# Moving a ring's rows and indices: from copies on GpSimd to DMAs issued by SyncE, in a graph network with residual norms

## The reference

```python
x = _layernorm(x + _L0_gnn_ref(x, src, dst))                 # 10 steps of propagation, alpha = 0.1
x = _layernorm(x + _L1_gnn_ref(x, edge_index, w, fc_w, fc_b, bias))   # attention, 4 heads
x = _layernorm(x + _L2_gnn_ref(x, ..., src, dst, edge_type_86))       # 16 basis matrices by type
x = _layernorm(x + _L3_gnn_ref(x, edge_weight, edge_index, 100000))   # weighted sum over edges
```

## Time and profile before

| | |
|---|---|
| median of three runs | 2988.89 us |
| the profiled execution's own time | 2987.88 us |
| its span, first to last instruction | 2986.1 us |
| DVE busy | 2053.3 us, 69% |
| POOL busy | 1783.6 us, 60% |
| ACT busy | 574.2 us, 19% |
| PE busy | 536.1 us, 18% |
| chain that ended last | DVE 39%, issue 22%, POOL 13%, DMA 6%, PE 5%, ACT 3% |
| POOL's copies out of the ring (L716) | 40 into YW, 14.6 us; 12 into RB, 9.3 us |
| DMA queues | POOL's 7.0%, SP's 6.7% of 16 engines' span |

### The profile page before, as it was taken

One profiled execution on the slowest core, in us unless ns is written; L12 is line 12 of the kernel. 1 busy time (PEld: TensorE's weight loads), 2 busy tenths in 40 slices (PEclk: granted clock), 3 DMA queues, 4 the chain that ended last, 5 costly groups with the idle time before them and its releaser, 6 DMA issues.

```text
span 2986.1 us, 24643 instructions
## 1 busy us (share of the span) xinstructions
PE 536.1 (18%) x3578; PEld 339.1 (11%) x3578; DVE 2053.3 (69%) x3755; ACT 574.2 (19%) x1342; POOL 1783.6 (60%) x1893
## 2 busy tenths in 40 slices
PE   4760000047100000000003022320245450000000
PEld 2330000036100000000002011220122220000000
DVE  6777878878863555555899377069778788676662
ACT  6970111113000000000012002431233330101000
POOL 5777777777735265556557777670346460715776
PEclk9995555569555555555556555555555555555555
DMA  6002222200011022222120101011000001000000
GB/s 210 13 12 86 76 72 76 66 22 13 12 55 11 20 21 23 26 20 53 55 52 10 52 11 8 1 52 44 4 6 7 6 8 44 10 2 7 10 9 9
DMA packets 78886, 96.54 MB, mean 32 GB/s; under 512 B 45888, under 2 KB 70640, under 8 KB 76920
## 3 DMA queue, kind: packets, MB, share of 16 engines
q0 software_dynamic: 53664, 20.91, 7.0%
q1 hardware_dynamic: 25176, 75.21, 6.7%
HBM read 38.06 MB, written 60.81 MB: 33 GB/s over the span
## 4 chain that ended last, share of the span: by engine, by line
DVE 39%; issue 22%; POOL 13%; DMA 6%; PE 5%; ACT 3%; DVEq 2%; POOLq 1%; ACTq 1%; SPq 0%
POOL ring L724 4%; POOL cring L465 3%; DMA cring<-sums_by_list,cidx 2%; DVE YW L1180 2%; DVE RB L1180 1%; POOL attention_by_edge L820 1%; PE banks L2580 1%; POOL out_dram L481 1%; POOL ring L813 1%; DVE YW L1017 1%; DVE YW L1011 1%; DVE roots L1008 1%; DVE roots L1018 1%; DVE roots L1012 1%; DVE SW L1300 1%
## 5 line engine op out<-in xcount | busy, mean ns | idle before, releaser
L481 POOL DMA_INDIRECT out_dram<-ring,ridx x196 | 206.1, 1051 | 141.5 <-DVE ridx L2074 82.6
L490 POOL DMA_INDIRECT SW<-node_table,srci x196 | 220.8, 1126 | 64.5 <-issue 64.5
L490 POOL DMA_INDIRECT XS<-in_x_dram,xsi x196 | 202.1, 1031 | 81.6 <-issue 62.3
L490 POOL DMA_INDIRECT XD<-in_x_dram,xdi x196 | 202.7, 1034 | 62.6 <-issue 62.6
L839 POOL DMA_INDIRECT out_dram<-z4w,oidx x98 | 96.2, 982 | 225.2 <-ACT oidx L2334 195.6
L465 POOL DMA_INDIRECT cring<-sums_by_list,cidx x128 | 123.6, 966 | 120.4 <-issue 78.8
L2132 ACT ACT_TABLE_LOAD x42 | 53.9, 1283 | 641.6 <-DVEq L997 641.6
L2367 PE MATMUL banks<-YW 128*128 128x392 f16 x784 | 140.2, 333 | 47.5 <-ACT YW L2154 37.6
L2449 PE MATMUL banks<-tl,dcar 128*128 128x32 f32 (+1 forms) x14 | 4.4, 404 | 799.4 <-DVEq L1290 618.3
L724 POOL DMA_INDIRECT ring<-x_by_edge,aidx x96 | 95.1, 990 | 41.9 <-issue 22.5
L942 DVE TENSOR_SCALAR YW<-YW,b_d 128x784 f16<-128x784 f16 x196 | 83.0, 424 | 49.0 <-PE banks L2367 47.1
(11 more groups left out here) (614 smaller groups left out, 3420.8 us busy)
## 6 DMA issues: line engine op xcount, KB each, us to landing
nx<-in_x_dram SPq DMA_DIRECT2D x10, 625.0 KB
YW<-in_x_dram SPq DMA_DIRECT2D x10, 625.0 KB
out_dram<-nx SPq DMA_DIRECT2D x10, 625.0 KB
out_dram<-YW SPq DMA_DIRECT2D x10, 625.0 KB
sums_by_list<-RB SPq DMA_DIRECT2D x2, 1800.0 KB
sums_by_edge<-RB SPq DMA_DIRECT2D x1, 3528.0 KB, 9.8
sums_by_list<-RB SPq DMA_DIRECT2D x2, 1600.0 KB
XS<-in_x_dram,xsi POOLq DMA_INDIRECT x196
```

The source lines that it names most:

```text
L481: pool.indirect_dma_start(out=table, out_offset=off, in_=ring_row(h, j, w), in_offset=None, bounds_check=limit, oob_is_err=False).then_inc ...
L490: pool.indirect_dma_start(out=dest[:, t * w:(t + 1) * w], out_offset=None, in_=table, in_offset=bass.IndirectOffsetOnAxis(ap=idx[:, t:t + ...
```

## The change

POOL's `fetch_rows` and `put_rows` lose their copies: POOL waits for `moved_s` (or `staged_s`) and issues the indirect DMAs, nothing else. The copies become plain DMAs that SP issues from two new functions: `fetch_moves` writes the landed rows from the ring to the target tile and the next indices into aidx, `put_moves` writes indices and rows into aidx and the ring. A semaphore per half counts 16 for each of these DMAs. SP waits for each half's landing itself.

```diff
+            def fetch_moves(n, idx, dest, moved_s, landed_s, k=0):
+                width = 2 * CU * D
+                def index(h, i):
+                    sp.dma_start(aidx[:, h, 0:CU], idx[:, bass.ds(i * (2 * CU) + h * CU, CU)]).then_inc(moved_s[h], 16)
+                def rows(h, at_, landed):
+                    sp.wait_ge(landed_s[h], landed)
+                    sp.sem_inc(s_tick[4], 1)
+                    sp.dma_start(dest[:, bass.ds(at_, CU * D)], ring[:, h, 0:CU * D]).then_inc(moved_s[h], 16)
+                for h in range(2):
+                    index(h, 0)
+                with sp.Fori(1, n) as i:
+                    for h in range(2):
+                        rows(h, i * width + (h * CU * D - width), (n * (16 * CU) + i * (16 * CU)) if k else i * (16 * CU))
+                        index(h, i)
+                for h in range(2):
+                    rows(h, n * width + (h * CU * D - width), n * (16 * CU * (k + 1)))
+            def put_moves(n, idx, rows, w, staged_s, put_s):
+                def stage(h, i):
+                    sp.dma_start(aidx[:, h, 0:CU], idx[:, bass.ds(i * (2 * CU) + h * CU, CU)]).then_inc(staged_s[h], 16)
+                    sp.dma_start(ring[:, h, 0:CU * w], rows[:, bass.ds(i * (2 * CU * w) + h * (CU * w), CU * w)]
+                                 ).then_inc(staged_s[h], 16)
+                for h in range(2):
+                    stage(h, 0)
+                with sp.Fori(1, n) as i:
+                    for h in range(2):
+                        sp.wait_ge(put_s[h], i * (16 * CU))
+                        sp.sem_inc(s_tick[4], 1)
+                        stage(h, i)
+                for h in range(2):
+                    sp.wait_ge(put_s[h], n * (16 * CU))
+                    sp.sem_inc(s_tick[4], 1)
...
@@ SP's program behind the ten steps
-            write_table(agg_d, 1)
...
             sp.dma_start(e4w[:, :], inv_d.rearrange("(p j) w -> p (j w)", p=P)).then_inc(s_invl, 16)
+            write_table(agg_d, 1)
+            sp.wait_ge(s_tabw, 16)
+            fetch_moves(n0, rows0, YW, s_fst, s_fget)
             sp.wait_ge(s_x1, 1)
             sp.dma_start(dense(x1_d, D), XD[:, :]).then_inc(s_x1w, 16)
+            sp.wait_ge(s_trips[3], 1)
+            ns = sp.value_load(trips_i[3][0:1, 0:1], min_val=1, max_val=CW // (2 * CU))
+            sp.wait_ge(s_qi, 1)
+            fetch_moves(ns, qi, SRD, s_srt[0], s_sget[0])
+            sp.wait_ge(s_agu, 1)
+            fetch_moves(ns, si, SRS, s_srt[1], s_sget[1])
             sp.wait_ge(s_sgo, SINGLES)
             sp.dma_start(dense(att_d, D), S[:, :]).then_inc(s_gw, 16)
...
+            sp.wait_ge(s_dup, 1)
+            put_moves(ns, ti, SA, D, s_tset, s_tput)
             sp.dma_start(S[:, :], dense(attd_d, D)).then_inc(s_attl, 16)
-            for h in range(2):
-                sp.wait_ge(s_dput[h], ns * (16 * CU))
-                sp.sem_inc(s_tick[4], 1)
+            put_moves(ns, qi, SA, D, s_dset, s_dput)
             sp.dma_start(Y, dense(att_d, D)).then_inc(s_al, 16)
             write_table(rgcn_d, 2)
+            sp.wait_ge(s_tabw, 32)
+            fetch_moves(n0, rows0, YW, s_fst, s_fget, 1)
@@ POOL
+            def fetch_rows(n, table, moved_s, landed_s, k=0):
+                with pool.Fori(0, n) as i:
+                    for h in range(2):
+                        pool.wait_ge(moved_s[h], (n * 32 + (i * 32 + 16)) if k else (i * 32 + 16))
+                        pool.sem_inc(s_tick[0], 1)
+                        for j in range(CU):
+                            pool.indirect_dma_start(out=ring_row(h, j, D), out_offset=None, in_=table, ...
+            def rows_moved(moved_s, count): ...   # waits for both halves' moves
+            def put_rows(n, w, table, staged_s, put_s, last): ...   # likewise, waits for i * 32 + 32
```

More of the change, by code:

```diff
@@ L371, in gnn_resnorm @@
         s_x1, s_x1w = sem("x1_dst_ready"), sem("x1_dst_written")
-        s_srt = [sem(f"sorted_{side}_staged") for side in ("dst", "src")]
+        s_srt = [[sem(f"sorted_{side}_moved{h}") for h in range(2)] for side in ("dst", "src")]
         s_sget = [[sem(f"sorted_{side}_landed{h}") for h in range(2)] for side in ("dst", "src")]
@@ L409, in gnn_resnorm @@
         s_expl = sem("list_values_loaded")
-        s_stg = [sem(f"group_staged{k}") for k in range(2)]
-        s_xtp = [sem(f"group_transposed{k}") for k in range(2)]
-        s_xtc = [sem(f"transposed_group_copied{k}") for k in range(2)]
+        s_stg = [None, sem("group_staged")]
+        s_xtp = [None, sem("group_transposed")]
+        s_xtc = [None, sem("transposed_group_copied")]
         s_xy, s_xyu = sem("relation_terms_ready"), sem("relation_terms_used")
@@ L707, in _ @@
             pool.sem_inc(s_tick[0], 1)
[L708 to L714, removed]
-                    pool.sem_inc(s_tick[0], 1)
[L716 to L726, removed]
-                plus = lambda a, b: a + b if k else b
-                for h in range(2):
-                    issue(h, 0, plus(step0, h + 1))
-                with pool.Fori(1, n) as i:
-                    for h in range(2):
-                        take(h, i * width + (h * CU * D - width), plus(get0, i * (16 * CU)))
-                        issue(h, i, plus(step0, i * 4 + 2 * h))
-                for h in range(2):
-                    take(h, n * width + (h * CU * D - width), n * (16 * CU * (k + 1)))
@@ new lines, in fetch_rows @@
+            def fetch_rows(n, table, moved_s, landed_s, k=0):
[4 more added lines that the diff above has]
+                        for j in range(CU):
+                            pool.indirect_dma_start(out=ring_row(h, j, D), out_offset=None, in_=table,
+                                                    in_offset=bass.IndirectOffsetOnAxis(ap=aidx[:, h, j:j + 1], axis=0)
+                                                    ).then_inc(landed_s[h], 16)
@@ new lines, in rows_moved, with put_rows @@
+            def rows_moved(moved_s, count):
+                for h in range(2):
+                    pool.wait_ge(moved_s[h], count)
+                    pool.sem_inc(s_tick[0], 1)
+            def put_rows(n, w, table, staged_s, put_s, last):
+                with pool.Fori(0, n) as i:
+                    for h in range(2):
+                        pool.wait_ge(staged_s[h], i * 32 + 32)
+                        pool.sem_inc(s_tick[0], 1)
+                        for j in range(CU):
+                            pool.indirect_dma_start(out=table, out_offset=bass.IndirectOffsetOnAxis(
+                                ap=aidx[:, h, j:j + 1], axis=0), in_=ring_row(h, j, w), in_offset=None,
+                                bounds_check=last, oob_is_err=False).then_inc(put_s[h], 16)
@@ L765, in put_rest @@
                     pool.sem_inc(s_tick[0], 1)
-            def put_rows(n, idx, rows, w, table, staged_s, put_s, last):
-                trip = put_trips(idx, rows, w, table, staged_s, put_s, last)
-                trip(0, first=True)
-                put_rest(trip, 1, n, put_s)
             put_dup = put_trips(drow, dupay, 4, inv_d[:, :], s_pset, s_pput, P * CW - 1)
@@ L1819, in listed_rows @@
             def listed_rows(m):
-                dve.wait_ge(s_fst, trips0 * (4 * m))
-                dve.sem_inc(tick, 1)
+                for h in range(2):
+                    dve.wait_ge(s_fst[h], trips0 * (32 * m))
+                    dve.sem_inc(tick, 1)
                 expand(Y3)
@@ L1857, in logits @@
             def logits(rows, k, z):
-                dve.wait_ge(s_srt[1 - k], ns * 4)
-                dve.sem_inc(tick, 1)
+                for h in range(2):
+                    dve.wait_ge(s_srt[1 - k][h], ns * 32)
+                    dve.sem_inc(tick, 1)
                 shape = [P, 2 * CU, NH, D]
```

27 lines of the change are left out of this document (13 added, 14 removed).

## The result

The changed kernel takes 2960.35 us (median of 4 runs, 2959.40 to 2960.85); the kernel before, timed beside it, 2988.65 us (4 runs, 2988.18 to 2989.51). The ratio is 0.9904, 95% interval [0.9891, 0.9918]: 28.3 us faster. The forecast was 2958 us, with a range of 2948 to 2978. The profiled execution of the changed kernel has a span of 2958.5 us against 2986.1, 27.6 us less.

The account below looks back on a forecast made before the run. DVE's three waits for POOL from 1440 us on were taken to bound the kernel. Gains of 22.2 us up to the load of S and 8.9 in the last fetch, 31.1, took 2988.89 to 2958 us; range 2948 to 2978.

Parts of the forecast that it names:

- Step 1: Dst-side fetch: 12 halves 0.94 us shorter each, +11.3, less 1.3 for a slower hand-over to the src fetch; together +10.0 us.
- Start of the dst fetch, taken as unchanged: The write of XD comes from DVE, which nothing speeds up; first index moves land with it: no gain.
- Step 2: Src-side fetch: 12 halves at 0.94 us, +11.3; last rows arrive by a move, -1.5; DVE's products start 19.8 us earlier.
- Step 3: Before the attention trips: attention_table's write now stands behind both fetches in SP's order, POOL waits 9.8 us, -9.6 us.
- Attention trips, left at 0: POOL keeps its +11.7 us through them; fewer slow indirects beside DVE's products might give up to 4 us more, not counted.
- Step 4: First attention put: cold start -1.3 us, 12 halves at 0.98 us, +11.8; the load of S starts 22.2 us earlier.
- Step 5: Second put: indices queue behind the load of S, start some 10.5 us after its issue; cost nothing, cover 30 us.
- The stretches taken to shift as a whole: Later work, such as that between 2060 and 2520 us, was let shift as a whole.
- Step 6: Last fetch: start -1.3, 14 halves at 0.94 us, +13.2, last rows by a move -1.5, two uncovered trips -1.5; together +8.9 us.
- Rival A: Near 1600 us, DVE's lock on POOL goes with the copies: 5.7 us more gained, 2952 us; chance 0.12.
- B to D: SP's moves land slower: at 3.4 us, 2972 us (chance 0.15); at 5.0, 3018 us (0.10); at about 4.0, 2989 us (0.05).
- m: Time of SP's second DMA in a half's turn, issue to landing: taken as 1.8 us, hidden up to 3.1.

## Why the prediction was right, and where 3.5 us of it were not

Three things held: the stretches in which DVE waits for POOL, the halves of 5.00 us with the moves hidden behind the other half, and the wait for attention_table's write. The second put cost nothing, as forecast. The sum came out at 31.1, the trace gives 27.6 and the medians 28.5 against the 2988.89 of the forecast. Step by step:

- **Step 1, dst fetch, +10.0.** Measured 78.52 - 70.90 = 7.6 (1548.01 to 1626.53 before, 1546.62 to 1617.52 after). From the first indirect to the last it is 74.68 before and 65.24 after, 9.4 us: 12 halves have 11 intervals between them, 11 x 0.94 = 10.3, less 0.8 for the held instruction, an indirect of 7.45 us in place of 0.95 where it was a copy of 6.01 in place of 0.29. (That part depends on the moment: in a second execution of the same kernel the held indirect took 6.30.) The hand-over to the src fetch, last indirect to first, went from 3.84 to 5.66: -1.8, not -1.3. The twelfth 0.94 stands for the copies ahead of the first indirect (1547.00 to 1548.01). They went, but "the first index moves, queued behind that write, land with it" was wrong: POOL goes on 10.64 us after the issue of XD's write (1535.98 to 1546.62), where it went on after 9.42 (1537.58 to 1547.00) and had its first indirect out after 10.43. So nothing was gained there.
- **Start of the dst fetch, taken as unchanged.** It came 1.4 us earlier. 0.7 of it was there already when the table write ahead of the fetch went out (1437.59 before, 1436.86 after), in code that the change leaves alone: luck, for the sum. The other 0.7 came behind that write, as in the run that has only the e4w load's new order.
- **Step 2, src fetch, +9.8 for DVE.** Measured 7.9 (78.43 to 70.49). One half was counted twice (0.94): the copies of the first half are those that the hand-over, 1.3 us, already holds. Another 1.0 us, net, is the trip that turned late at 1628.94, a wait of 1.74 us for its indices. A second execution of the same kernel has it too (2.04 us), and the run with the write on ScalarE's queue has 1.31 us, ahead of that write; five other kernels with the same src fetch have at most 0.57 us there. Packets of instruction loading pass at that time in kernels with the wait and without it, so the cause stays open.
- **Step 3, the write of attention_table, -9.6.** Measured 3.88 to 13.20 us from the last indirect to the attention trips' first, -9.3.
- **Attention trips, left at 0, "up to 4 us more, not counted".** +2.8, as shown above. This hid a part of the overcount.
- **Step 4, first put, -1.3 + 11.8.** The start measured -2.1 (from the end of the trips to the put's first indirect, 1.27 before and 3.33 after), and the put itself 75.44 - 64.41 = 11.0, again one half less, as its first copies are in the 1.3 us too. The load of S goes out 20.8 us earlier (22.2 predicted).
- **Step 5, second put, 0.** It started 12.1 us behind the load's issue (1921.72 to 1933.78), 10.5 predicted, and its load of Y went out at 1998.16 with DVE's want of it some 40 us later.
- **The stretches taken to shift as a whole.** They gave back 1.1 us: the load of S reached DVE 0.4 us later after its issue, the work up to the write of rgcn_table took 0.4 us longer, the work behind the last fetch 0.2. No run tells these from the scatter of single executions.
- **Step 6, last fetch, +8.9.** Measured 104.60 - 96.72 = 7.9; the miss is one half, 0.94, counted twice as in steps 2 and 4. The run of this segment alone has 7.8.

The balance: one half too many in each of four segments, 3 x 0.94 + 0.98 = 3.8 us; 0.8 for the held instruction, 1.0 at the hand-overs and the put's start, 1.0 for the late trip and 1.1 in the stretches behind are 3.9 more. Against these 7.7 us stand 2.8 of the attention trips and 1.4 of the earlier start. That leaves 3.5, so the forecast is this close partly by luck.

**Rival A** is out: the indirect at 1597.84 took 7.45 us inside DVE's 6.69 us instruction of 1597.78. A lock of that kind does not go with the copies. SP's own issues inside the same instruction, at 1597.83 and 1598.46, took their usual 0.50 and 0.51 us. **B to D** are out by m = 1.8 to 1.9 as landed. Their price was too low, though: with a cover of 0.5 us in place of 1.3, B's m = 3.4 would have cost 25 x 1.1 + 6.4 = 34 us by estimate, more than the whole gain. That error made no difference to the time, because m came out where it was taken. For the Trainium skill's fixed cost (DMA: Bandwidth & Descriptors, Anatomy of one DMA), about 2.0 us, which the page gives for DMAs that POOL issues, the 1.9 us of SP's 2 KB moves agree within 0.1, and the 64 KB ones land under it in 1.8.

## What to carry to other kernels

When an engine's small copies are moved to a queue, count intervals, not items: the first copy of each burst is in the hand-over already. Set one engine's time for the other half against the whole turn (landing, issues at 0.50 us, landing again), and test the cover with a run in which the turn is longer; inside it moves are free, beyond it each trip pays the excess. And a transfer that is pulled forward out of a wait must be checked for what it then runs beside: here a 3 MB write shortened one wait by 7.6 us, and only 1.0 us of that was left at the first put.

## What the runs showed that was not expected

- A 3136 KB write on another engine's queue holds SyncE's small moves all the same: POOL waited 7.41 us where the write landed 9.6 us after its issue at 1640.60, and 5.48 us in the other run that has the write there.
- SP's moves out of the ring take 0.50 us each to issue and those into it 0.51, against 0.33 to 0.36 for most transfers of 3136 KB. The four that follow each other at the start of a put take 0.50 to 0.63, and the 3136 KB write of attention_table, directly behind two moves, took 0.58.
- The moves that land in 1.8 to 1.9 us do so whether they carry 2 KB or 64 KB over the same 128 partitions.
